# Feature interaction on one core: block-diagonal weights, transposes next to weighing, single-partition stores of the last row pairs, eight staging slots

## What is computed

```python
B, F, E = 2048, 200, 64           # r_feature (B, F, E), weight (F, E, E)
bilinear = jnp.einsum('bie,ied->bid', feature, weight)
out = jnp.einsum('bid,bjd->bij', bilinear, feature)   # (2048, 200, 200)
```

## Time and profile before

| | |
|---|---|
| runs, median of 3 | 1572.7 us |
| profiled execution | 1573.6 us |
| its span, first to last instruction | 1571.8 us |
| TensorE busy | 1525.3 us |
| VectorE busy | 1145.3 us |
| ScalarE busy | 928.2 us |
| mean granted TensorE clock | 0.996 of 2.4 GHz |
| moved by DMA | 438.51 MB, 279 GB/s |
| queue of SP, share of 16 engines | 89.8% |

### The profile page before, as it was taken

How to read it: one execution, slowest core, us unless ns; L and a number is a source line. 1 busy time by engine, 2 the same in 40 slices (tenths; PEclk the granted TensorE clock), 3 DMA queues, 4 the chain that set the end, 5 groups by cost and what they waited for, 6 DMA issues and landing times.

```text
span 1571.8 us, 40835 instructions
## 1 busy us (share of the span) xinstructions
PE 1525.3 (97%) x16192; PEld 1209.0 (77%) x16192; DVE 1145.3 (73%) x2048; ACT 928.2 (59%) x1313; POOL 0.7 (0%) x6
## 2 busy tenths in 40 slices
PE   8999999999999999999999999999999999999974
PEld 6888778877788777887778877788777887788753
DVE  0567777777777778678787687777777777786896
ACT  5666556655566655665556655566555665556532
POOL 0000000000000000000000000000000000000000
PEclk9999999999999999999999999999999999999998
DMA  9788999889989999989999899899999989999788
GB/s 234 226 270 267 297 295 282 280 268 293 296 275 288 281 293 283 292 275 277 288 289 292 274 281 296 275 289 280 290 290 283 286 273 290 288 280 289 239 266 248
DMA packets 294235, 438.51 MB, mean 279 GB/s; under 512 B 38049, under 2 KB 242849, under 8 KB 294049
## 3 DMA queue, kind: packets, MB, share of 16 engines
q1 hardware_dynamic: 294048, 435.92, 89.8%
HBM read 108.13 MB, written 327.68 MB: 277 GB/s over the span
## 4 chain that ended last, share of the span: by engine, by line
PE 88%; DVE 8%; issue 2%; DMA 1%; SPq 0%; ACT 0%; DVEq 0%
PE ps L219 49%; PE bp L203 24%; PE tp L187 14%; DVE staging L250 4%; DVE win L298 2%; DVE win L305 1%; PE ps L203 1%; PE ps L187 1%; DMA x<-feature_dram 0%; DMA out_dram<-staging 0%; DVE win L306 0%; SPq L138 0%; SPq L131 0%; ACT staging L250 0%; ACT bl L272 0%
## 5 line engine op out<-in xcount | busy, mean ns | idle before, releaser
L219 PE MATMUL ps<-win,bl 64*100 64x200 f32 x8192 | 932.3, 354 | 24.1 <-DVE staging L250 23.9
L219 PEld LDWEIGHTS ps<-win,bl 64*100 64x100 f32 x8192 | 699.7, 207 | 167.6 <-issue 164.7
L250 DVE COPY staging<-ps 100x800 f32<-100x800 f32 x512 | 505.8, 988 | 326.7 <-PE ps L219 324.6
L272 ACT COPY bl<-bp 128x512 f32<-128x512 f32 x384 | 322.3, 839 | 449.7 <-PE bp L203 449.7
L250 ACT COPY staging<-ps 100x800 f32<-100x800 f32 x512 | 423.1, 826 | 164.9 <-PE ps L219 162.9
L203 PE MATMUL bp<-xt,w 64*64 64x128 f32 x6144 | 419.7, 276 | 0.0
L203 PEld LDWEIGHTS bp<-xt,w 64*64 64x64 f32 x6144 | 326.8, 133 | 83.5 <-ACT xt L263 78.7
L298 DVE COPY win<-xt 128x400 f32<-128x400 f32 x512 | 276.7, 541 | 63.4 <-ACT xt L263 47.5
L187 PE MATMUL tp<-ident,x 128*128 128x128 f32 x1536 | 252.8, 287 | 5.9 <-DMA x<-feature_dram 5.9
L187 PEld LDWEIGHTS tp<-ident,x 128*128 128x128 f32 x1536 | 161.6, 141 | 89.3 <-issue 89.1
L263 ACT COPY xt<-tp 128x512 f32<-128x512 f32 x384 | 226.6, 590 | 5.3 <-PE tp L187 5.3
(11 more groups left out here) (4 smaller groups left out, 0.4 us busy)
## 6 DMA issues: line engine op xcount, KB each, us to landing
out_dram<-staging SPq DMA_DIRECT2D x1024, 300.0 KB, 4.1
x<-feature_dram SPq DMA_DIRECT2D x400, 256.0 KB, 4.1
out_dram<-staging SPq DMA_DIRECT2D x512, 25.0 KB
w<-weight_dram SPq DMA_DIRECT2D x24, 128.0 KB, 5.6
w<-weight_dram SPq DMA_DIRECT2D x2, 64.0 KB, 4.4
```

The source lines that it names most:

```text
L219: last = nc.tensor.matmul(ps[s % TILES][0:FH, h, F * b:F * (b + 1)], rows_of_bl(n, R * k + PB * i + b)[64 * h:64 * h + 64], win[64 * h:64 ...
L250: copy(staging[:, slot, :, :, :].rearrange("p b h j -> p h b j"), ps[s % TILES][0:FH, :, 0:PB * F].rearrange("p h (b j) -> p h b j", j=F)) ...
L272: nc.scalar.copy(group_of_bl(n, t), bilinear_tile(n, t).rearrange("p (c b) -> p c b", c=C)).then_inc(bl_stored, 1)
```

## The change

The diff is shown without its assertions on sizes.

```diff
@@ -32,14 +32,15 @@
     QUADS = NB // R
     PB = 2
     SETS_B = NB // PB
-    XSLOTS = 6
+    XSLOTS = 5
     TILES = 3
-    OSLOTS = 12
-    WSLOTS = 4
+    OSLOTS = 8
+    REST = 4
+    WSLOTS = 3
     WG = 2
     FA = FH // 16 * 16
     feature_v = feature.rearrange("b f e -> b (f e)")
     weight_v = weight.rearrange("(m h) e d -> h e m d", h=2)
@@ -62,7 +63,7 @@
-        w = sbuf("w", [128, FH, E])
+        w = sbuf("w", [128, FH, 2 * E])
         ident = sbuf("ident", [128, 128])
         x = sbuf("x", [128, XSLOTS, 2 * C * E])
         xt = sbuf("xt", [128, QUADS, QUADS, C, R])
@@ -81,6 +82,7 @@
         x_loaded = [sem(f"x_loaded{i}") for i in range(XSLOTS)]
         ident_zero = sem("ident_zero")
         ident_ready = sem("ident_ready")
+        w_zero = sem("w_zero")
         transposed = sem("transposed")
         xt_stored = sem("xt_stored")
         bilinear_done = sem("bilinear_done")
@@ -91,7 +93,7 @@
         staged_act = sem("staged_act")
         staged_dve = sem("staged_dve")
         out_written = [sem(f"out_written{i}") for i in range(OSLOTS)]
-        rest_written = [sem(f"rest_written{i}") for i in range(OSLOTS // 2)]
+        rest_written = [sem(f"rest_written{i}") for i in range(OSLOTS // REST)]
         block = ctx.enter_context(nc.Block())
@@ -110,7 +112,7 @@
         def group_of_bl(n, t):
             if n % 2 == 0:
                 return bl[:, C * t:C * (t + 1), :]
-            return bl[:, :, C * t:C * (t + 1)].rearrange("p b c -> p c b")
+            return bl[:, :, C * t:C * (t + 1)]
         def rows_of_bl(n, b):
             return bl[:, 0:FH, b] if n % 2 == 0 else bl[:, b, 0:FH]
@@ -135,18 +137,22 @@
             def load_w(i):
                 ms = slice(WG * C * i, min(WG * C * (i + 1), FH))
                 for h in range(2):
-                    sp.dma_start(w[64 * h:64 * h + 64, ms, :], weight_v[h, :, ms, :]).then_inc(w_loaded[i], 16)
+                    sp.dma_start(w[64 * h:64 * h + 64, ms, E * h:E * (h + 1)], weight_v[h, :, ms, :]).then_inc(w_loaded[i], 16)
             def store(s):
                 slot = s % OSLOTS
                 wait_staged(sp, s)
                 sp.dma_start(out_v[0:FA, PB * s:PB * (s + 1), :], staging[0:FA, slot]
                              ).then_inc(out_written[slot], 16)
-                if s % 2:
+                if s % REST == REST - 1:
                     wait_staged(sp, s - 1)
-                    sp.dma_start(out_v[FA:FH, PB * (s - 1):PB * (s + 1), :],
-                                 staging[FA:FH, slot - 1:slot + 1].rearrange("p s b h j -> p (s b) (h j)")
-                                 ).then_inc(rest_written[slot // 2], 16)
+                    for p in range(FA, FH):
+                        sp.dma_start(out_v[p:p + 1, PB * (s + 1 - REST):PB * (s + 1), :],
+                                     staging[p:p + 1, slot + 1 - REST:slot + 1].rearrange(
+                                         "p s b h j -> p (s b) (h j)")
+                                     ).then_inc(rest_written[slot // REST], 16)
             for t in range(NG + XSLOTS):
                 if t % WG == 0 and t < NG:
@@ -163,8 +169,8 @@
             for slot in range(OSLOTS):
                 uses = (BLOCKS * SETS_B - slot + OSLOTS - 1) // OSLOTS
                 sp.wait_ge(out_written[slot], 16 * uses)
-                if slot % 2:
-                    sp.wait_ge(rest_written[slot // 2], 16 * uses)
+                if slot % REST == REST - 1:
+                    sp.wait_ge(rest_written[slot // REST], 16 * (FH - FA) * uses)
         @block.gpsimd
         def _(pool):
@@ -173,6 +179,7 @@
             nc.gpsimd.affine_select(out=ident[:], in_=ident[:], compare_op=ALU.not_equal, fill=1.0,
                                     base=0, pattern=[[-1, 128]], channel_multiplier=1
                                     ).then_inc(ident_ready, 1)
+            nc.gpsimd.memset(w[0:64, :, E:2 * E], 0.0).then_inc(w_zero, 1)
         @block.tensor
         def _(pe):
@@ -192,6 +199,7 @@
                 at = n * NG + t
                 pe.wait_ge(xt_stored, at + 1)
                 if n == 0:
+                    pe.wait_ge(w_zero, 2)
                     pe.wait_ge(w_loaded[t // WG], 32)
                     if t >= 3:
                         pe.wait_ge(bl_stored, t - 2)
@@ -199,11 +207,8 @@
                     pe.wait_ge(bl_stored, at)
                 features = group_of_xt(n, t)
                 for c in range(C):
-                    for h in range(2):
-                        last = nc.tensor.matmul(bilinear_tile(n, t)[64 * h:64 * h + 64, NB * c:NB * (c + 1)],
-                                                w[64 * h:64 * h + 64, C * t + c, :],
-                                                features[64 * h:64 * h + 64, :, c, :],
-                                                start=True, stop=True)
+                    last = nc.tensor.matmul(bilinear_tile(n, t)[:, NB * c:NB * (c + 1)], w[:, C * t + c, :],
+                                            features[:, :, c, :], start=True, stop=True)
                 last.then_inc(bilinear_done, 1)
             def scores(n, k, i):
@@ -234,9 +239,9 @@
             for n in range(BLOCKS):
                 for k in range(QUADS):
                     scores(n, k, 0)
+                    scores(n, k, 1)
                     if k in transposed_at and (n + 1) * NG + transposed_at[k] < BLOCKS * NG:
                         transposes((n + 1) * NG + transposed_at[k])
-                    scores(n, k, 1)
                     if k in weighed_at and n + 1 < BLOCKS:
                         bilinear(n + 1, weighed_at[k])
@@ -246,7 +251,7 @@
             used = s // OSLOTS
             if used:
                 engine.wait_ge(out_written[slot], 16 * used)
-                engine.wait_ge(rest_written[slot // 2], 16 * used)
+                engine.wait_ge(rest_written[slot // REST], 16 * (FH - FA) * used)
             copy(staging[:, slot, :, :, :].rearrange("p b h j -> p h b j"),
                  ps[s % TILES][0:FH, :, 0:PB * F].rearrange("p h (b j) -> p h b j", j=F)
                  ).then_inc(staged, 1)
@@ -269,7 +274,8 @@
                 if n:
                     act.wait_ge(scores_done, (n - 1) * SETS_B + 2 * t + 2)
-                nc.scalar.copy(group_of_bl(n, t), bilinear_tile(n, t).rearrange("p (c b) -> p c b", c=C)
+                cells = "p (c b) -> p c b" if n % 2 == 0 else "p (c b) -> p b c"
+                nc.scalar.copy(group_of_bl(n, t), bilinear_tile(n, t).rearrange(cells, c=C)
                                ).then_inc(bl_stored, 1)
             store_xt(0)
@@ -306,6 +312,7 @@
                 nc.vector.tensor_copy(win[0:64, slot, :, 2:F + 1:2], win[64:128, slot, :, 1:F + 1:2]
                                       ).then_inc(win_filled, 1)
+            nc.vector.memset(w[64:128, :, 0:E], 0.0).then_inc(w_zero, 1)
             LAST = BLOCKS * QUADS
             for q in range(WSLOTS - 1):
                 fill_own(q)
```

More of the change, by code:

```diff
@@ L41, in feature_interaction @@
     assert 2 * E == 128 and B % NB == 0 and FH % C == 0 and NG <= QUADS and R == 2 * PB
-    assert PB * F <= 512 and C * NB == 512 and OSLOTS % 2 == 0
+    assert PB * F <= 512 and C * NB == 512 and OSLOTS % REST == 0 and (BLOCKS * SETS_B) % OSLOTS == 0
     feature_v = feature.rearrange("b f e -> b (f e)")
```

## The result

The changed kernel took 1896.33 us in the median of 4 runs (1895.84 to 1896.9), the kernel before 1573.39 (1572.21 to 1574.11) beside it. The ratio is 1.2054, its 95% interval 1.2033 to 1.2074: a fifth slower. The forecast of 1466 and the range up to 1548 were wrong, and so was the direction. The profiled execution took 1895.99 for a span of 1894.2.

The account below looks back on a forecast made before the run. TensorE was taken to bound the kernel, with DMA within 33 us. TensorE falls from 1571.8 by 143, plus 12 for windows, to 1441; fullest DMA engines at 1456 plus 9 give span 1465, median about 1466, range 1438 to 1548.

Parts of the forecast that it names:

- Stores: SP's queue: 512 more issues, two quads taking 3.6 to 6.0 of 6.1 us, so SP keeps up.
- The bound beside TensorE: Fullest DMA engines by bytes at equal time per byte: 1539 us busy before, 1456 with eight engines per small store.
- rival 1: DMA limited by bytes at 290 GB/s, not by the fullest engine; only the slow parity gains: 1534 us, chance 0.20.
- TensorE: Fewer entries between kinds of work save 0.35 or 0.42 us per quad, 143 us in all; TensorE alone ends at 1429.
- Rival 2: On TensorE, going from transposes to weighing still pays an entry: 1502 us, chance 0.14.
- My sign for rival 2: Transpose group followed by weighing after 0.44 us as forecast; 0.59 would show the rival.
- Three windows: One window fewer between VectorE and TensorE: 0.8 us waiting 15 times, 12 us, bounds 0 and 25.
- Start: GpSimd zeroing w, at most 10.2 us, hidden by loads: 0 us, bounds -3 and +5.
- Engines per small store: Each single-partition, eight-row store uses eight DMA engines, giving 44,193 small packets (37,025 if one engine).
- Eight slots: Staging slots freed by fours: landing 5.2 to 8.3 us against 8.3 until ScalarE needs the slot, cover 0 to 3.
- Rival 3: Single-partition stores run slowly, eight engines reading one partition: about 2010 us, spread from 1572 to over 2000, chance 0.13.

Follow-up runs that it names:

- spread singles: Kernel before, 12 slots, with single-partition stores of eight rows, one behind each large store of the next four sets instead of four in a row: 1696.85 us.
- the two-by-two kernel: Kernel before with each small store split into two DMAs of two partitions and four rows: 1679.83 us, ratio 1.0681.
- the first two kernels: Changed kernel with four-partition small stores: one per four sets, slots freed by fours, 1639.12 us; one per two sets, freed by twos, 1531.94 us.

## Why the prediction was wrong

**The step that failed** is "Stores": "3.6 to 6.0 us of the 6.1 of two quads. The medians hold waiting for full queues, so I take it that SP keeps up." Measured, two quads of SP's issues are 7.40 us (and its lower end adds up to 3.5, not 3.6). It failed in three ways.
- The size. I took the issue of the new form from the four-partition store (minimum 0.26). One partition and eight rows has a minimum of 0.62, and 0.87 in the row above. No row of before showed this form; a bound from both sides, up to the 0.91 of the small store in the earlier trace rows, would have given 4 x 0.46 + 4 x 0.9 + 2 x 0.73 = 6.9 us, already over 6.1 and, times 256, 1766 us. The term was priced at nothing for want of this bound.
- What the waiting means. I read the medians over the minima as waiting that goes away. They did not go away: span less waits, SP spends 0.60 us on an issue before, 0.61 with 512 more cheap ones, 0.64 with spread singles and 0.67 in the changed kernel. 512 more cheap ones took 340 us of SP and cost the kernel 99 and 107, with 404 us of waiting beside them at the start. Nor is that length a property of the shape. It is 0.50 without small stores, 0.74 with one small store per four sets and 0.81 where ScalarE issues them, and there the large store's median is 0.76 where it is 0.45 in the slower kernel with one queue. What stretches an issue is not in the profile.
- The row of four. That the engines run dry while SP is busy with small work was in no step. Spreading the same stores saved 205 us.

**Where the 329 us went** (1573 to 1902, form alone, on the kernel before): 99 for 512 more issues, 25 more in the kernel with spread singles (1697 against 1672; by the two-by-two kernel 17), and 205 for standing in a row. These are differences between kernels, and they need not add up in another order. The changed kernel's gain at TensorE, 41 us with one queue, is hardly to be seen behind it: 1896 against 1902.

**The bound beside TensorE.** I put it at the fullest DMA engines, 1539 us before and 1456 after. The kernel with ScalarE's queue moves the same output in small stores of four engines each (38,048 small packets) in 1471 us, below 1539. By the same working its fullest engines would be busy (0.904 + 0.040) x 29.7/27.2 = 103% of the span, which can't be. So a premise is wrong, equal time per byte or the same four engines for every small store; the trace doesn't name the engines, and which premise fails stays open. The 290 GB/s before were no limit of bytes either (rival 1): that kernel moves 301 through 90 us. The new order gains 41 us with the small stores on SP's queue and 61 more with them on ScalarE's. I had read "SP issues back to back" in the earlier trace rows and gone on to the engines.

**TensorE** came as forecast: a quad is 0.89 + 1.64 + 0.59 = 3.12 us for 3.50 and 0.89 + 1.53 + 0.59 = 3.01 for 3.32, where I had 3.08 and 2.97. Rival 2 (transposes to weighing pays an entry) would leave weighing at about 1.02. The kernel without small stores has both cases, weighing after a transpose and, at quad 28, weighing after scores (timeline, start and length):

```profile
837.12 1.06 PE L199 MATMUL bp<-xt,w 128*128 128x128 f32 x8
838.11 3.11 PE L213 MATMUL ps<-win,bl 64*100 64x200 f32 x32
841.15 1.16 PE L199 MATMUL bp<-xt,w 128*128 128x128 f32 x8
842.27 1.71 PE L213 MATMUL ps<-win,bl 64*100 64x200 f32 x16
```

From start to start it is 0.99 us after a transpose and 1.12 after scores, so the entry is 0.13 and is not paid after a transpose. In the first block, where no scores stand between, a pair of transposes and weighing takes 1.33 us where no load holds it (1.61 before). My sign for rival 2, a transpose group of 0.59 instead of 0.44, was wrong: the group still comes after scores and pays its own entry, as my own quads of 3.08 and 2.97 had it. The Trainium skill, TensorEngine Tiling (Array Packing), section Key Properties, says that changing the tiling mode drains TensorE and changing the tile alone does not; the 0.89 after a transpose agrees, since both now work on the whole array. The floor without small stores is 1456.6, 15 above my 1442 for TensorE with three windows. Weighing is 0.04 us dearer than I had it (0.89 for 0.85), and over 360 quads that is 14 us, nearly all of the 15.

**Three windows** I had at 12 us, at most 25. In the kernel without small stores TensorE's weight loads wait for VectorE's windows, the last block included:

```profile
PEld ps L213 <- DVE win L300: 58.4, 74, 1.0
```

No run has four windows in the new order, so their price isn't shown. **Start**: each half of w was zeroed in 5.4 us and no wait for it reached the path; the first scores start at 48.5 us instead of 50.3. **Engines per small store**: 44,192 small packets, 44,193 forecast; eight engines each. **Eight slots**, at a cover of 0 to 3 us and no cost, hold when freed in pairs in the kernel before (1574), but not when freed by fours: 107 us between the first two kernels. The form's cost masks it in the changed kernel: 12 slots with the same stores, in the kernel before, take no less (1902).

**Rival 3** had the right sign and size (about 2010, from 1572 on) by another mechanism: packets that read one partition slowly. The pages speak against it. Packets took 0.898 x 1571.8 = 1411 us of an engine in the mean before and 0.759 x 1894.2 = 1438 in the changed kernel, 26 more; if eight engines had it all, that is 52 us each, where rival 3 needs 106 to matter and 552 for its 2010. On GpSimd's queue the same output rows run in a kernel of 1531 us and land after 3.7. I had given the sign 0.12.

**Open.** Why one partition and eight rows takes 0.62 us to issue and 16 rows 0.51; what SP waits for inside an issue, so that one takes 0.6 us and more where its minimum is 0.24 to 0.32; whether a second queue helps by the issues it takes off SP or by what it can have under way beside SP's; how the 107 us of the freeing by fours divide; what the lower clock (0.93) costs in the changed kernel, since it came with the waiting and was not varied.

## What to carry to other kernels

Price a queue as an engine: the number of issues times the length they have in a full stretch of the timeline, not the minimum or the median (here 4.4 and 5.2 us against 7.40). Where a new shape has no row, take the longest issue seen as the upper bound. A queue that issues back to back in the profile is suspect before anything is added to it, even while another engine holds the chain. Small DMAs in a row starve the engines of large ones, so spread them or give them to another queue. Judge slots by how many come free at once, against the time a store needs to land.

## What the runs showed of the hardware

The shortest issue on SP depends on the shape: 4 partitions by 4 rows 0.26 us, 2 by 4 0.24, 96 by 2 0.32, 1 by 16 0.51, 1 by 8 0.62. How long an issue takes in the run is another matter: the 96 by 2 has a median of 0.45 in the changed kernel and 0.76 with the small stores on ScalarE. On ScalarE 4 by 4 takes 0.26 in the median too, and on GpSimd, where the profile counts it as busy time, 0.57 (1 by 8: 0.52).

A second queue shortened a kernel by 61 us (1532 to 1471) and by 366 (1896 to 1531) at the same output. The Trainium skill, DMA: Bandwidth & Descriptors, section "Issuing engines are not separate DMA queues", says that issuing from several engines saves only the sequencer's time to initiate, "which is usually small relative to the DMA itself". Here it was not small beside the run: SP's time in issues fell from 1315 to 1173 us and the run by 61, and the rate went from 287 to 298 GB/s. That only this time was saved is not shown.
